# Attention pairs taken from one batch, and the last stage's work on batch 0 spread over the MLP chunks of a Swin block with self-attention

## The reference

```python
# layer 0: windows of 8 x 8 tokens, 16 heads of 8 channels
xn = layer_norm(x, norm1_g, norm1_b)
xw = windows(roll(xn, -4, -4))                     # 4 * 16 windows, 64 tokens each
q, k, v = heads(xw @ qkv_w.T + qkv_b)
q, k = rope2d(q), rope2d(k)
attn = softmax(q * 8**-0.5 @ k.T + attn_mask[window])   # mask: 0 or -100, one per window of the image
x = x + roll(unwindow((attn @ v) @ proj_w.T + proj_b), 4, 4)
y = layer_norm(x, norm2_g, norm2_b)
a, gate = split(y @ fc1_w.T + fc1_b)               # 2 x 512
x = x + (silu(gate) * a) @ fc2_w.T + fc2_b
# layer 1: in every batch, N = 1024 tokens, f and g have 16 channels
f, g, h = x @ Wq + bq, x @ Wk + bk, x @ Wv + bv
beta = softmax(f @ g.T)                            # 1024 x 1024 per batch
out = gamma * (beta @ h) + x
```

## Time and profile before

| | us |
|---|---|
| median of 3 runs | 422.26 (419.81 to 424.24) |
| the profiled execution, its own time | 421.29 |
| its span, first to last instruction | 419.5 |
| busy in the span: PE / VectorE / ScalarE / GpSimd | 363.6 / 307.5 / 275.2 / 259.1 |
| granted TensorE clock, mean | 0.966 |

### The profile page before, as it was taken

How to read it: one execution, slowest core, us unless ns; L and a number is a source line. 1 busy time by engine, 2 the same in 40 slices (tenths; PEclk the granted TensorE clock), 3 DMA queues, 4 the chain that set the end, 5 groups by cost and what they waited for, 6 DMA issues and landing times.

```text
span 419.5 us, 12535 instructions
## 1 busy us (share of the span) xinstructions
PE 363.6 (87%) x4732; PEld 229.6 (55%) x4732; DVE 307.5 (73%) x850; ACT 275.2 (66%) x436; POOL 259.1 (62%) x313
## 2 busy tenths in 40 slices
PE   2678799999999999978799999999269998989693
PEld 0455455666665666655355555545025766767563
DVE  8767688888888888887476666645787688784524
ACT  2758787777787778878355555455116866768581
POOL 6656476777777777886656666572006775857521
PEclk9999999999999999999899999999757999999989
DMA  6701001111000101100000000000100002010101
GB/s 199 253 22 26 18 27 27 28 28 30 26 25 25 28 26 30 29 16 3 1 2 2 0 0 0 2 0 9 45 0 15 14 19 58 3 50 2 43 11 51
DMA packets 15581, 12.53 MB, mean 30 GB/s; under 512 B 3991, under 2 KB 14136, under 8 KB 15416
## 3 DMA queue, kind: packets, MB, share of 16 engines
q1 hardware_dynamic: 14144, 11.42, 9.4%
q10 hardware_dynamic: 1400, 0.61, 0.6%
HBM read 4.68 MB, written 2.10 MB: 16 GB/s over the span
## 4 chain that ended last, share of the span: by engine, by line
PE 55%; DVE 20%; issue 7%; ACT 6%; POOL 4%; DMA 4%; SPq 3%; ACTq 0%; DVEq 0%; POOLq 0%
PE ps L334 8%; PE ps L1417 7%; PE ps L786 5%; PE ps L758 5%; DVE mx L1553 4%; PE ps L748 4%; PE ps L843 3%; PE ps L1361 3%; PE ps L779 3%; PE ps L767 3%; DVE ps L973 3%; POOL hl L275 2%; DVE ob L1591 2%; PE ps L750 2%; PE ps L1400 2%
## 5 line engine op out<-in xcount | busy, mean ns | idle before, releaser
L1679 POOL TENSOR_TENSOR el<-e,eh 128x1024 f16<-128x1024 f32 x28 | 59.6, 2130 | 65.2 <-ACT eh L1671 65.0
L1162 POOL TENSOR_TENSOR p_lo<-e_buf,p_hi 128x1024 f16<-128x1024 f32 x32 | 68.2, 2132 | 4.9 <-ACT p_hi L1017 3.6
L1664 ACT ACTIVATE e<-ps 128x1024 f32<-128x1024 f32 x32 | 32.7, 1023 | 39.0 <-PE ps L1406 38.7
L334 PE MATMUL ps<-y_t,fc_w 128*128 128x512 f16 x192 | 44.4, 387 | 3.7 <-POOL al L260 2.5
L1154 POOL TENSOR_TENSOR rot<-ta,tb 128x256 f32<-128x256 f32 x32 | 23.3, 728 | 38.9 <-DVE tb L941 38.7
L1553 DVE TENSOR_REDUCE mx<-ps 128x1 f32<-128x1024 f32 x32 | 39.1, 1221 | 9.9 <-PE ps L1390 9.6
L1417 PE MATMUL ps<-val,eh 128*128 128x129 f16 x512 | 37.7, 223 | 6.4 <-DVE ob L1591 5.7
L758 PE MATMUL ps<-mask,identb 128*128 (+1 forms) x128 | 39.0, 386 | 2.8 <-DMA k_t<-qk_t 2.1
L973 DVE TENSOR_REDUCE ps<-ps 128x16 f32<-128x1024 f32 x32 | 39.4, 1232 | 2.7 <-PE ps L767 1.8
L1081 ACT ACTIVATE e_buf<-ps 128x1024 f32<-128x1024 f32 x32 | 32.8, 1025 | 12.9 <-PE ps L779 12.8
L1417 PEld LDWEIGHTS ps<-val,eh 128*128 128x128 f16 x512 | 32.4, 99 | 15.0 <-issue 8.4
(11 more groups left out here) (158 smaller groups left out, 981.7 us busy)
## 6 DMA issues: line engine op xcount, KB each, us to landing
k_t<-qk_t SPq DMA_DIRECT2D x128, 32.0 KB, 1.8
x_all<-in_x SPq DMA_DIRECT2D x8, 256.0 KB, 5.6
out<-ob SPq DMA_DIRECT2D x8, 192.0 KB, 2.1
mask_f<-in_mask SPq DMA_DIRECT2D x1, 1024.0 KB, 4.8
yr<-xr SPq DMA_DIRECT2D x14, 64.0 KB, 2.0
fc_w<-in_fc_w SPq DMA_DIRECT2D x1, 512.0 KB, 6.8
out<-ob SPq DMA_DIRECT2D x4, 128.0 KB, 1.8
fc_w<-in_fc_w SPq DMA_DIRECT2D x1, 256.0 KB, 6.6
```

What stands on the lines that cost most here:

```text
L334: last = pe.matmul(ps[:, bank, :], fc1_w16[:, ws, 128 * block_:128 * block_ + 128], y_t[:, v, ys, :], start=(n == 0), stop=(n == 2))
L1162: pool.tensor_tensor(p_lo[:, u], e_buf[:, u], p_hi[:, u], ALU.subtract).then_inc(plo_done, 1)
L1679: pool.tensor_tensor(el[:, T % H_BUFS, :], e4[:, T % E_BUFS, :], eh[:, T % H_BUFS, :], ALU.subtract).then_inc(el_done, 1)
```

## The change

1. **Pairs.** A pair is now two neighbouring windows of one batch, so chunks 0 and 1 are batch 0, chunks 2 and 3 batch 1, and so on. The mask is stored for 8 pairs of windows and not twice for 16 windows (512 KB and not 1024 KB), and repeats after 8 pairs; so the attention loop has 2 passes of 8 steps (8 to 23), with 8 steps written out ahead of it, and the mask has a fixed address.
2. **The MLP is written out** for c = 1 to 9.
3. **A bank is freed.** For chunks after 3 `turn_a` writes to the bank of `project` (5), and waits for `x1_ready`; bank 4 (`FIRST_BANK`) is free from `body(3)` on.
4. **Batch 0 in the MLP.** In `body(3)`: the factors `gbv` and `fg_bm`, and the rows of batch 0. In `body(4)` to `body(7)`: four halves of a score tile each, one matmul into bank 4 and one maximum of 512 columns per half (16 in all; slots 0, 1, 2 behind `fc1(k)`, slot 3 ahead of `fc2(0)`). In `body(8)`: the 8 maxima are put together (`first_maxima`), the rows of batch 1 made, the maxima turned, the values of batch 0 made, and the exp table loaded.
5. `pads` moves from the end of `body(7)` to the end of `body(2)`. AHEAD is 9; tile 8 is made in step T = 0. All copies `yr` are issued by SP.

In this diff, `first_batch` stands three times: for TensorE, VectorE and ScalarE, in this order.

```diff
-        AT_BANK, PRJ_BANK, YT_BANK, OUT_BANK = 4, 5, 0, 7
+        PRJ_BANK, YT_BANK, OUT_BANK = 5, 0, 7
+        FIRST_BANK, FIRST_CHUNK = 4, 3
+        def at_bank(c):
+            return FIRST_BANK if c <= FIRST_CHUNK else PRJ_BANK
+        def first_halves(c, slot):
+            if FIRST_CHUNK < c < CHUNKS and slot < 4:
+                return (4 * (c - FIRST_CHUNK - 1) + slot) // 2, slot % 2
+            return None
...
+            def first_batch(c, slot):
+                if c == FIRST_CHUNK and slot in (0, 2):
+                    h = slot // 2
+                    pe.wait_ge(x2_done, h + 1)
+                    wait(pe, fg_ready, h)
+                    project_fg(pe, 0, h)
+                tile = first_halves(c, slot)
+                if tile is not None:
+                    n, half = tile
...
+                    wait(pe, half_max, 2 * n + half)
...
+                    pe.matmul(ps[:, FIRST_BANK, :], left, right, start=True, stop=True).then_inc(half_done, 1)
+                if c == CHUNKS:
...
                 if in_range(c, 1):
                     for k in range(HBLK - 1):
...
+                        first_batch(c, k)
...
+            def first_batch(c, slot):
+                if c == FIRST_CHUNK and slot in (0, 2):
+                    if slot == 0:
+                        factors(dve)
+                    rows_of(dve, 0, slot // 2)
+                tile = first_halves(c, slot)
+                if tile is not None:
+                    n, half = tile
+                    dve.wait_ge(half_done, 2 * n + half + 1)
+                    dve.tensor_reduce(mxh[:, n, half:half + 1], ps[:, FIRST_BANK, :], AX.X, ALU.max, negate=True)\
+                        .then_inc(half_max, 1)
...
+            def first_batch(c, slot):
+                if c == FIRST_CHUNK and slot in (0, 2):
+                    if slot == 0:
+                        act.wait_ge(pads_set, PADS + 2)
+                    high_rows(act, 0, slot // 2)
+                if c == CHUNKS:
+                    if slot < 2:
+                        high_rows(act, 1, slot)
+                    if slot == 3:
+                        act.activation(warm4[:], gbv[:, 0:1], ACT.Exp)
+                    if slot in (3, 4):
+                        high_values(act, 0, slot - 3)
...
-            LOOP_FROM, LOOP_TO = 4, PAIRS - 4
+            LOOP_FROM, LOOP_TO = WPAIRS, PAIRS - WPAIRS
...
-        E_BUFS, H_BUFS, LAG, AHEAD = 3, 4, 2, 10
+        E_BUFS, H_BUFS, LAG, AHEAD = 3, 4, 2, 9
...
-    x = x.reshape(B, nh, WIN, nw, WIN, DIM).transpose(1, 3, 0, 2, 4, 5).reshape(PAIRS, 2 * WTOK, DIM)
+    x = x.reshape(B, nh, WIN, nw, WIN, DIM).transpose(0, 1, 3, 2, 4, 5).reshape(PAIRS, 2 * WTOK, DIM)
```

More of the change, by code:

```diff
@@ L506, in body @@
                     residual_sum(c, u)
-                if in_range(c, 1) and not first:
+                if in_range(c, 1) and c > 1:
                     hidden(c - 1, 0)
@@ new lines, in v_bank, with tokens, project_fg, four_tiles @@
+        def v_bank(b, h):
+            return (PRJ_BANK, YT_BANK)[h] if b == 0 else AUX
+        def tokens(b, first, count):
+            return x2_all[:, b * NB + first:b * NB + first + count]
+        def project_fg(pe, b, h):
+            pe.matmul(ps[:, fg_bank(b, h), :], fg_w[:], tokens(b, 512 * h, 512), start=True, stop=True)\
+                .then_inc(fg_done, 1)
+        def four_tiles(pe, b, h, bank, right):
+            for k in range(4):
+                last = pe.matmul(ps[:, bank, 128 * k:128 * k + 128], tokens(b, 512 * h + 128 * k, 128), right,
+                                 start=(k == 0), stop=True, skip_group_check=True)
+            return last
@@ new lines, in project_v, with turn_maxima, factors @@
+        def project_v(pe, b, h):
+            four_tiles(pe, b, h, v_bank(b, h), wv[:]).then_inc(v4_done, 1)
+        def turn_maxima(pe, b, bank):
+            pe.wait_ge(mh_ready, b * BT + BT)
+            out = ps[:, bank, :].bitcast(F16)
+            for n in range(BT):
+                last = pe.transpose(out[:, 128 * n:128 * n + 128], mh[:, b % 2, n, :], ident16[:])
+            last.then_inc(mt_done, 1)
+        def factors(dve):
+            dve.wait_ge(pads_set, PADS)
+            dve.tensor_scalar(gbv[:], bv[:], cols[:, 1:2], None, ALU.mult).then_inc(pads_set, 1)
+            dve.tensor_scalar(fg_bm[:], fg_b[:, 0:1], fg_b[:, 1:2], None, ALU.mult).then_inc(pads_set, 1)
@@ new lines, in high_values, with mlp_steps, _ @@
+        def high_values(act, b, h):
+            act.wait_ge(v4_done, 2 * b + h + 1)
+            wait(act, pv4_done, (b - 1) * BT)
+            act.activation(val[:, b % 2, 0, 4 * h:4 * h + 4, 0:DIM],
+                           ps[:, v_bank(b, h), :].rearrange("p (n d) -> p n d", n=4), ACT.Copy,
+                           scale=VSCALE).then_inc(v4_hi, 1)
+        def mlp_steps(eng, body):
+            for c in range(1, CHUNKS + 2):
+                body(c, c % 2)
+        @block.gpsimd
+        def _(pool):
+            body, early = mlp_pool(pool)
+            mlp_steps(pool, body)
@@ new lines, in by_vector, with wait_low, other_half @@
+        def by_vector(key):
+            return key >= TILES - BT and key % 2 == 1
+        def wait_low(eng, key):
+            if by_vector(key):
+                eng.wait_ge(el_last, (key - TILES + BT) // 2 + 1)
+            elif key >= 0:
+                eng.wait_ge(el_done, key + 1 - max(0, key - TILES + BT + 1) // 2)
+        def other_half(eng, b, h, side):
+            eng.wait_ge(fg_ready, fg_count(b, h))
+            part = slice(512 * h, 512 * h + 512)
+            rows, other = slice(64 * side, 64 * side + 64), slice(64 - 64 * side, 128 - 64 * side)
+            eng.dma_start(yr[rows, b % 3, part], xr[other, b % 3, part]).then_inc(y_ready[b % 3], 16)
@@ new lines, in _ @@
+        @block.scalar
+        def _(act):
+            for T in range(TILES):
+                b, n = T // BT, T % BT
+                act.wait_ge(st4_done, T + 1)
+                wait_low(act, T - E_BUFS)
+                act.activation(e4[:, T % E_BUFS, :], two(ST4), ACT.Exp).then_inc(exp4_done, 1)
+                if n in (2, 3) and b + 2 < B:
+                    high_rows(act, b + 2, n - 2)
+                if n in (4, 5) and b + 1 < B:
+                    high_values(act, b + 1, n - 4)
+                act.wait_ge(exp4_done, T + 1)
+                wait(act, pv4_done, T - H_BUFS + 1)
+                act.activation(eh[:, T % H_BUFS, :], e4[:, T % E_BUFS, :], ACT.Copy).then_inc(eh_done, 1)
@@ L1709, in _rope_tables @@
+            for b in range(B):
+                if b >= 1:
+                    store(b - 1)
+                if b + 2 < B:
+                    for h in range(2):
+                        for side in range(2):
+                            other_half(sp, b + 2, h, side)
+            store(B - 1)
+            for u in range(2):
+                sp.wait_ge(stored[u], 48 * (B // 2))
 def _rope_tables():
```

780 lines of the change are left out of this document (358 added, 422 removed).

## The result

The changed kernel takes 411.56 us (median of 4 runs, 409.99 to 412.22) against 421.91 (4 runs, 419.81 to 424.24): ratio 0.976, 95% interval 0.9721 to 0.9799. It is faster, but by 10.4 us and not by the 17.2 that I forecast; 405.0 was 6.6 us too low, and 411.56 lies just outside the range of 400.5 to 411.5. The profiled execution took 412.08 with a span of 410.2.

The account below looks back on a forecast made before the run. It took a serial ramp of 22.99 us before the last stage as the removable cost, with the MLP barely bound by TensorE. Terms summed to -17.2, from the median 422.26 to 405.0 us; range 400.5 to 411.5.

Parts of the forecast that it names:

- Loops: -1.0 and -1.9: MLP and attention loops: written-out MLP chunks save 1.0 us, four fewer attention jumps of 0.48 us save 1.9.
- The start, -1.0: Kernel start: 0.5 MB less mask lands bv 1.4 us earlier, its matmuls start 1.3 earlier; gain 1.0 us.
- The ramp, -23.0: Between MLP and last stage's pipeline: the serial 22.99 us of projections, maxima and transposes is removed whole.
- the first steps, -1.2: Steps T = 0 to 2 of the last stage: 9.4 us against 10.6, with tiles 8 to 10 made there.
- chunk 3: MLP chunk 3: two added projections and waits on memsets, factors and rows cost 3.0 us, bounds +1.7 and +4.5.
- Chunks 4 to 7, +4.2: MLP chunks 4 to 7: four half-score matmuls and maxima each cost 1.05 us per chunk, 4.2 in all.
- rival 1: Score halves in MLP: one bank is too narrow, 16 slots wait 0.5 us longer, 413 us; chance 0.15.
- Chunk 8, +3.5: MLP chunk 8: added projections, values and transposes on TensorE cost 3.5 us, bounds +2.5 and +4.5.
- Rival 2: New waits in chunks 3 to 7 lower TensorE's clock, making the kernel slower, about 430 us and more; chance 0.03.
- a lower clock: Sign of being wrong: TensorE's granted clock under 1.00 in the MLP after 210 us.
- Rival 3: MLP cheaper than thought: chunks 4 to 7 cost 2.4 us, chunk 3 2, chunk 8 2.5; 401 us; chance 0.10.
- Rival 4: Ramp does not go: a late stamp holds the first scores_turned, some 6 us stay, 411 us; chance 0.04.

Follow-up runs that it names:

- b_loop8: Kernel before with only its attention loop made 8 steps long, 2 passes (steps 8 to 23): 422.84 us against 421.59, ratio 1.0023.
- a_unroll: Changed kernel with no attention loop, all 37 step bodies written out for all engines: 414.85 us against 411.56.
- a_latewait: Changed kernel with TensorE's wait for the copies of K moved behind the two mask matmuls of the scores: 404.88 us, ratio 0.9602.
- b_latewait: Kernel before with TensorE's wait for the copies of K moved behind the two mask matmuls: 420.02 us against 420.95, ratio 0.9973.
- a_twice: Changed kernel with each of the 16 half-score matmuls issued twice into the same bank: 414.15 us in one run.

## Why the prediction was wrong

**The step that failed is "Loops: -1.0 and -1.9"**, in its attention part. I counted four jumps less, 4 x 0.48, and took written-out code as free, since "steps written out at the end are no slower (4.7 to 4.8)". That reading was of a few steps that happened to be good; in the two steps after them, at 178.85 and 183.69, the same trace had two waits for k_t of 0.47 and 0.48 us, in written-out code, and a third at 37.69 in the first steps. I gave such waits no term. The change takes the number of step bodies that run for the first time from 17 to 29. The jumps were indeed saved (steps 16 to 23 take 4.76 to 4.80 in a row after), and the copies of K were late in ten places. In the two traces the way from the first to the last maximum grew by 4.9 us (157.18 to 162.11), where 1.9 less was forecast: 5.4 us more of waits, less 1.9 for the jumps, and about 1.4 that I put down to the clock, an estimate by what is left. The medians bear this out in size, not in each part: the loop alone, put into the kernel before, is worth 3.1 us against the forecast (b_loop8), and the late wait takes 5.8 us out of what the change had added, with 1.5 to 3 us of uncertainty in each; what the clock adds by itself no run shows. The Trainium skill has the rule that I had cited (Runtime: NRT & Kernel Launch, section Instruction fetch mechanics): straight code is streamed, and a taken branch out of the window stalls. From it I had taken that written-out code costs nothing, and that did not hold: b_loop8 gained nothing by four jumps less (+1.2 us, with -1.9 expected), and a_unroll lost 3.3 with one jump less. TensorE did not stall for its own code in either (neither has an entry "issue" in its waits); the loss came by the copies. With the late wait in both kernels the change is worth 15.1 us of the 17.2. Of the 2.1 that are left about 1 is the terms below, and the rest still lies in the attention, which takes 156.67 us from the first to the last maximum in a_latewait and 156.85 in b_latewait, with 1.9 less forecast.

**The start, -1.0**, was right in size, and for these two traces by luck. The first maximum came 1.01 us earlier, but bv let TensorE go only 0.16 us earlier (19.36 in the earlier trace rows, 19.20 now), not 1.3. The rest is a shorter gap behind it, 1.69 before and 0.98 after. Before:

```profile
24.62 0.80 PE L748 MATMUL ps<-qkv_w,xn_all 128*128 128x256 f16 x3 [1.69 <-issue]
```

After:

```profile
19.20 3.57 PE L491 MATMUL ps<-g1b,fc_w 128*128 128x1 f32 x16 [1.16 <-DMA bv<-in_bv]
23.74 0.80 PE L856 MATMUL ps<-qkv_w,xn_all 128*128 128x256 f16 x3 [0.98 <-DVE fc_bias L631]
```

Over all the traces the mechanism is nearer to what I had: the matmuls that wait for bv start at 19.36 to 20.07 in the eight with 1024 KB of mask and at 18.27 to 19.20 in the nine with 512 KB. The gain was then covered by the loss behind it.

**The ramp, -23.0, the first steps, -1.2, and chunk 3** were right in size and in mechanism. Chunk 3 took 14.15 us against 11.58, +2.57; the forecast was 3.0 less the 0.43 that an unrolled chunk saves. The order of waits was as written: VectorE's timeline in it reads

```profile
230.18 0.33 DVE L1418 TENSOR_SCALAR gbv<-bv,cols 128x128 f32<-128x128 f32 x1 [0.83 <-POOL val L332]
230.42 0.20 DVE L1419 TENSOR_SCALAR fg_bm<-fg_b 128x1 f32<-128x1 f32 x1
231.46 0.75 DVE L1427 SCALAR_TENSOR_TENSOR xr<-ps,fg_b,fgh 128x512 f16<-128x512 f32 x1 [0.84 <-ACT fgh L1451]
```

**Chunks 4 to 7, +4.2**, was mis-sized: +1.42 each in three chunks and +1.19 in the last, 5.4 in all. The bank wait that I put at 0.5 is 0.20 (rival 1's mechanism is there once per chunk, and small); the matmul that I put at 0.22 costs 0.32 and ends the fc1 run ahead of it 0.07 later, since it changes the rows from 128 to 64 and back (a_twice). The 4 x 0.39 + 0.20 - 0.27 = 1.49 of TensorE's own path is the chunk's 1.42. VectorE's path, which I had 0.9 late, did not hold TensorE up: no wait of TensorE for GpSimd's last lower part is left in the chunk. **Chunk 8, +3.5**, came out at 3.3.

**The rivals.** The time of rival 1, 413, was nearly hit, but in another stage and by another wait: the number would have led a reader astray. Rival 2 was half right, a clock that falls after a wait, but at 36 to 56 us in the attention and not in the new waits of chunks 3 to 7. In the MLP it was low once, at 208 to 212, as in the kernel before at 200 to 208, and 1.00 from there on. That reaches past 210, where I had named a lower clock as a sign of being wrong, but the kernel before has it too. Rival 3 is refuted by the 5.4. Rival 4 did not occur. A rival for new code had no place among them. That the range ended only 0.06 us short is of no weight: the mechanism was missing from it.

## What to carry to other kernels

When a change writes out a loop or makes it longer, count the bodies that run for the first time, and look in the old trace for what already waits in such code: those waits multiply with the bodies, while the jumps that are saved are visible and small. Place a wait for a DMA directly ahead of the first instruction that needs the data: moving it behind 0.6 us of independent work was worth 6.7 us in the changed kernel, where a copy had about 0.2 us of slack and many came late, and 0.9 in the kernel before, where few did. Compare the time before and after by stage first: the moved work was forecast within about 1 us, and the loss lay where the diff seemed to do only housekeeping.
